# The end of a two-layer decoder kernel: last attention group transposed earlier, last norms on VectorE, clip gate by the exponential, gated rows quantised in pairs of chunks without GpSimd

## The chip, the cores and the metric

The kernel runs on one core of a Trainium2 chip. The metric is the device time of one execution in microseconds (us). The time given for a kernel is the median of several runs.

The engines go by the profile's names: PE is the matrix engine (PEld its weight loads), DVE the vector engine, ACT the scalar engine, POOL is GpSimd, and SP issues the DMAs. Each engine works off its own list of instructions in order, and waits on semaphores where it needs another's result.

## The reference

Eight sequences of 100 rows of 256 numbers pass six sublayers, each followed by a residual sum and a layer norm. Only the last two touch the change.

```python
# fifth: attention of 100 rows over 361 context rows, 16 heads of 16, with a mask
x = _layernorm(x + _L1_xattn_ref(x, ctx_1024, ctx_1024, mask, ...), axis=-1)
# sixth: feed-forward part with 8-bit fake quantisation
def _act_fake_quant(x, clip_factor):
    scale = jax.nn.sigmoid(clip_factor) * jnp.max(jnp.abs(x)) / QMAX      # QMAX = 127
    return jnp.clip(_ste_round(x / scale), -QMAX - 1.0, QMAX) * scale
xq = _act_fake_quant(x, clip_x[0])
gate = jnp.einsum('bsh,ih->bsi', xq, _weight_fake_quant(w_gate))          # 256 -> 704
up = jnp.einsum('bsh,ih->bsi', xq, _weight_fake_quant(w_up))
h = _act_fake_quant(jax.nn.silu(gate) * up, clip_down[0])
x = _layernorm(x + jnp.einsum('bsi,hi->bsh', h, _weight_fake_quant(w_down)), axis=-1)
```

Both scales need the largest absolute value over all 800 rows: nothing of `xq` exists before the last row of the attention is normed, and nothing of the quantised `h` before the last piece of `silu(gate) * up`.

## The kernel before, in words

Everything is written out by hand for each engine. Only the end of the program matters here.

**The last attention.** 16 heads in 8 sequences make 32 groups ("quads", n = 0 to 31) of four heads. In step n PE computes the scores of quad n (`pe_scores`), then the product of probabilities and values of quad n-2 (`pe_values`), then work set by the table `AT` (keys, values, queries, output product), and last the twelve transposes of the probabilities of quad n-1 (`pe_probs`, L741) in three parts into three PSUM banks. ACT computes the exponentials of quad n (L945, one per head, with row sums) and copies the three parts of quad n-1 out of PSUM (`act_probs`, L954). When the last head of a sequence b has its sum, DVE inverts the 16 sums spread to 256 columns (`dve_inverse`, L1182 and L1183), PE turns the inverse into columns (`pe_spread`, called RS below), ACT copies it (L1047), and when the last `pe_values` of the sequence is done DVE multiplies both (`dve_context`, L1191). The output product (`pe_o`, operand `wo`), the residual sum (L1261) and the norm follow. The steps after quad 31 are n = 32 (values of 30, RS of the last sequence, transposes of 31), n = 33 (values of 31, output product, and the transposes of the quantised weights `pe_ffn_weights`, L2181 and L2190, which ACT copies out in L2237 and L2240) and n = 34 (the transposes FT of the last normed rows, L792, which ACT copies in L1039).

**A norm** is started by DVE (L618 to L620), its root is taken by POOL in six small steps (`norm_root`, L639 to L645), and it is ended by subtracting and multiplying: by DVE in `norm_end` (L652) in some places, by POOL in `norm_end_pool` (L658) in this attention.

**The feed-forward part.** The peak of a tensor over all partitions goes DVE, PE (L2197), DVE (L2324), PE, DVE (`activation_scale`, L2330 and L2332). The clip gate `clip` is the sigmoid of the two factors, taken by ACT (L2245) after the attention. DVE multiplies by the reciprocal scale and adds 12582912, which rounds, and clamps (L2351, L2352); ACT subtracts the constant again and writes bfloat16 (L2251). 16 chunks of 88 x 400 (two groups of 400 rows, eight chunks each) then pass PE (gate and up), ACT (Silu, L2257), DVE (product L2361, peak L2337). After the second peak each chunk is quantised: DVE scales and rounds (L2373), POOL clamps (L2278), ACT subtracts and writes `hq` in bfloat16 (L2263). PE starts on the first group's down product when its eight chunks are there (`f_hq`), 64 matrix products of 256 columns for 8 sequences. DVE takes the results in pairs of sequences, adds the residual and starts the norm; POOL takes the root and a shift (L2284, L2287); ACT ends the norm (L2270) and SP stores 100 KB for each sequence (L2124).

## Time and profile before

| | |
|---|---|
| runs of the kernel before, us | 1299.33, 1306.27, 1304.72; median 1304.72 |
| the profiled execution | 1300.62 us, its span 1298.9 us, mean granted PE clock 0.937 |
| busy over the span | PE 87%, DVE 82%, ACT 64%, POOL 60% |
| from the last scores (1225 us) to the end | 74 us |

The span runs from the first to the last instruction; the profiled execution's own time is 1.7 us more than its span. PEclk is the clock that PE was granted, 1.00 being 2.4 GHz and 0.50 being 1.2 GHz. The tiles `arena`, `ps`, `stat` and `x_tok` are the big SBUF arena, all of PSUM, the norm's numbers and the rows of the residual stream.

### The profile page before, as it was taken

What the parts mean: (1) busy time and instruction counts of PE and PEld (TensorE: products, weight loads), DVE (VectorE), ACT (ScalarE), POOL (GpSimd) and SP (SyncE); (2) the same over time, 40 slices, a digit from 0 to 9 for tenths busy, and PEclk for the clock granted to TensorE, in tenths of its full rate; (3) what the DMA queues carried; (4) which work ended last, traced back from release to release, by engine and by line L of the source; (5) the groups of instructions that cost most, each with busy time, mean ns of one, the idle gap of its engine ahead of it and who ended that gap; (6) DMA issues with size and microseconds to landing.
All of it is one profiled execution on the core that took longest, in us unless ns stands there. A gap on an engine that the chain in (4) does not pass through costs nothing.

```text
span 1298.9 us, 17433 instructions
## 1 busy us (share of the span) xinstructions
PE 1133.0 (87%) x5930; PEld 665.4 (51%) x5930; DVE 1060.2 (82%) x1629; ACT 831.1 (64%) x1827; POOL 785.5 (60%) x660
## 2 busy tenths in 40 slices
PE   7798988888768998998989989989997888989774
PEld 3455555544334554554545545545454556666544
DVE  4577777676699999999999999999999957675566
ACT  2455555655486677767766777677675447776754
POOL 6001111100599898998988989989999913543105
PEclk9899999979889998999998999989999899998975
DMA  6000002000510602305105024041060031010000
GB/s 209 13 12 13 12 13 73 1 1 3 205 38 10 239 1 103 118 1 196 52 1 203 17 80 169 1 179 42 1 236 1 1 83 33 17 34 2 1 2 25
DMA packets 22141, 79.13 MB, mean 61 GB/s; under 512 B 4935, under 2 KB 8847, under 8 KB 21138
## 3 DMA queue, kind: packets, MB, share of 16 engines
q1 hardware_dynamic: 22054, 78.02, 17.3%
q8 instruction: 48, 0.79, 0.3%
q14 instruction: 39, 0.32, 0.1%
HBM read 76.77 MB, written 1.24 MB: 60 GB/s over the span
## 4 chain that ended last, share of the span: by engine, by line
PE 40%; DVE 33%; POOL 11%; ACT 9%; issue 7%; DMA 0%; ACTq 0%; SPq 0%; DVEq 0%; POOLq 0%
PE ps L672 36%; DVE ps L2064 10%; POOL arena L1978 6%; DVE arena L2069 5%; DVE arena L2067 4%; PE ps L741 4%; POOL arena L1990 2%; DVE hstat L1197 2%; ACT ps L1861 2%; DVE arena L2027 2%; DVE arena L1174 1%; ACT L667 1%; ACT arena L930 1%; DVE arena L1164 1%; ACT arena L945 1%
## 5 line engine op out<-in xcount | busy, mean ns | idle before, releaser
L672 PE MATMUL ps<-arena 128*32 128x100 f32 (+8 forms) x3300 | 521.0, 386 | 71.4 <-ACT arena L930 14.8
L1978 POOL TENSOR_TENSOR arena<-arena 128x1600 f32<-128x1600 f32 x128 | 456.4, 3581 | 34.6 <-DVE ps L2064 26.4
L672 PEld LDWEIGHTS ps<-arena 128*32 128x32 f32 (+6 forms) x3300 | 263.1, 147 | 297.7 <-issue 116.3
L672 PE MATMUL ps<-arena,ident 128*128 128x400 f32 x1024 | 385.9, 527 | 29.7 <-POOL arena L1990 20.7
L1861 ACT ACTIVATE ps<-arena 128x400 f32<-128x400 f32 x512 | 282.9, 590 | 185.6 <-DVE arena L2067 152.4
L2064 DVE TENSOR_TENSOR_SCAN ps<-ps,arena 128x800 f32<-128x800 f32 x176 | 320.6, 1822 | 21.5 <-ACT ps L1861 17.5
L672 PEld LDWEIGHTS ps<-arena,ident 128*128 128x128 f32 x1024 | 201.2, 200 | 196.9 <-POOL arena L1990 29.1
L639 POOL TENSOR_SCALAR stat<-stat 100x1 f32<-100x1 f32 (+1 forms) x44 | 8.4, 190 | 394.3 <-DVE stat L620 393.4
L2067 DVE TENSOR_TENSOR arena<-ps,arena 128x800 f32<-128x800 f32 x176 | 174.3, 991 | 6.0
L1990 POOL TENSOR_TENSOR arena<-arena 128x1600 f32<-128x1600 f32 x40 | 143.1, 3577 | 16.9 <-DVE arena L2069 16.8
L2069 DVE TENSOR_TENSOR_SCAN arena<-ps,arena 128x800 f32<-128x800 f32 x80 | 140.3, 1803 | 1.4 <-ACT ps L1861 1.2
L954 ACT ACTIVATE arena<-ps 128x400 f32<-128x400 f32 x192 | 90.1, 502 | 23.3 <-PE ps L741 22.2
L945 ACT ACTIVATE arena<-arena,hstat 100x361 f32<-100x361 f32 x128 | 74.9, 588 | 39.0 <-DVE hstat L1174 39.0
L1174 DVE CUSTOM_DVE_ANT_0 arena<-ps,arena 100x361 f32<-100x361 f32 x128 | 60.6, 530 | 47.7 <-PE ps L672 47.7
L741 PE MATMUL ps<-ident,arena 100*128 100x100 f32 x768 | 93.7, 262 | 5.8 <-DVE arena L1321 2.4
L930 ACT ACTIVATE arena<-ps,hstat 100x361 f32<-100x361 f32 x128 | 71.5, 561 | 36.3 <-DVE hstat L1197 36.2
L741 PEld LDWEIGHTS ps<-ident,arena 100*128 100x128 f32 x768 | 79.2, 147 | 23.1 <-issue 9.2
L667 ACT ACT_TABLE_LOAD x65 | 83.4, 1283 | 1.1
L1197 DVE TENSOR_REDUCE hstat<-ps 100x2 f32<-100x722 f32 x64 | 57.8, 905 | 26.6 <-PE ps L672 26.2
L672 PE MATMUL ps<-wv,arena 128*128 128x256 f32 (+1 forms) x192 | 54.5, 411 | 4.0 <-DVE arena L1144 3.1
L672 PE MATMUL ps<-arena,wk 128*128 128x361 f32 x128 | 51.0, 527 | 1.5 <-ACT xm L1743 0.8
L1164 DVE TENSOR_SCALAR arena<-arena,hstat 100x361 f32<-100x361 f32 x128 | 46.5, 406 | 2.3
(196 smaller groups left out, 1023.2 us busy)
## 6 DMA issues: line engine op xcount, KB each, us to landing
arena<-bc_scratch SPq DMA_DIRECT2D x64, 800.0 KB, 6.6
arena<-in_ctxT SPq DMA_DIRECT2D x16, 361.0 KB, 4.0
arena<-in_w_in SPq DMA_DIRECT2D x4, 1024.0 KB, 5.2
arena<-in_expT SPq DMA_DIRECT2D x1, 2048.0 KB, 12.5
arena<-in_w_out SPq DMA_DIRECT2D x4, 512.0 KB, 3.1
arena<-in_mask SPq DMA_DIRECT2D x8, 141.0 KB
arena<-in_xT SPq DMA_DIRECT2D x2, 400.0 KB, 4.4
x_tok<-in_x_tok SPq DMA_DIRECT2D x1, 800.0 KB
```

Source lines behind the costliest of these rows:

```text
L667: act.add_instruction(mybir.InstLoadActFuncSet(name=nc.get_next_instruction_name(), act_func_set_id=which, engine=mybir.EngineType.Activat ...
L672: return nc.tensor.matmul(outp, lhsT, rhs, start=first, stop=last)
L741: last = nc.tensor.transpose(ps[:, a.bank(b, name), k * S:(k + 1) * S], a.es[0:S, (n * QUAD + i) % 8, kc * P:(kc + 1) * P], ident[0:S, 0:S])
L930: nc.scalar.activation(a.es[0:S, v % 8, 0:SK], ps[0:S, i, 0:SK], ACT.Exp, bias=hstat[0:S, n % 2, 0, i:i + 1], scale=1.0, accum_out=hstat[0 ...
L945: nc.scalar.activation(e, e, ACT.Exp, bias=hstat[0:S, n % 2, 0, i:i + 1], scale=-1.0, accum_out=rsum[0:S, n // QUADS % 2, sum_at(n, i)]).t ...
L954: nc.scalar.activation(a.aT[:, n % 2, r * QUAD * S:(r + 1) * QUAD * S], ps[:, a.bank(b, name), 0:QUAD * S], ACT.Copy).then_inc(a.freed(b, ...
L1861: last = nc.scalar.activation(psf[:, half_at(k) + j * GT:half_at(k) + (j + 1) * GT], delta[g][:, c], ACT.Exp, scale=aneg[:, l % 2, n:n + 1])
L1978: nc.gpsimd.tensor_tensor(bx[:, unit % BX].rearrange("p (j t) -> p j t", j=SEGMENT), bbc[:, nq].rearrange("p (j t) -> p j t", j=SEGMENT), ...
L1990: nc.gpsimd.tensor_tensor(h, h, cbc[:, nq], ALU.mult).then_inc(m_cmp, 1)
L2064: nc.vector.tensor_tensor_scan(a, a, bx[:, unit % BX, w], 0.0, ALU.mult, ALU.add).then_inc(m_scan, 1)
L2067: nc.vector.tensor_tensor(y, a, cbc[:, nq, w], ALU.mult).then_inc(m_cmd, 1)
L2069: nc.vector.tensor_tensor_scan(y, a, bx[:, unit % BX, w], 0.0, ALU.mult, ALU.add).then_inc(m_scan, 1)
```

## The change

It is four edits at the end of the program.

1. The transposes of quad 31 move from the end of step 32 to its start, ahead of the values of quad 30, on PE and on ACT; in step 31 ACT's copies of quad 30's transposes alternate with the exponentials of quad 31.
2. The last sequence's norm before the feed-forward part is ended by DVE instead of POOL, and so are the last two sequences of the output, where POOL's two shift instructions and ACT's L2270 fall away (SP waits on the new semaphore `f_ended`).
3. The clip gate becomes exp(-x) on ACT in step 8 of the attention, and 1/(1+that) in two small DVE instructions at the step of the third weight scale; the Sigmoid after the attention and its table load fall away. In the feed-forward part ACT writes both groups of `xq` before its first Silu.
4. The gated rows are quantised in 8 pieces of 88 x 800 instead of 16 of 88 x 400: DVE scales and rounds, ACT subtracts the constant and writes `hq`, and DVE clamps `hq` in bfloat16, two pieces behind. POOL has no part in it.

```diff
@@ -475,6 +475,9 @@
                     for n in LAST_QUADS:
+                        if n == B * QUADS:
+                            for r in range(KC):
+                                yield B - 1, f"T{QUADS - 1}{r}"
                         for g in quad_steps(n):
@@ -490,7 +493,7 @@
                                 yield b, "RS"
-                        if has_quad(n - 1):
+                        if has_quad(n - 1) and n < B * QUADS:
                             for r in range(KC):
@@ -870,6 +873,9 @@
                     pm_out(pe, ROUNDS - 1, n)
+                if n == B * QUADS:
+                    for r in range(KC):
+                        pe_probs(pe, a, n - 1, r)
                 if has_quad(n - 2):
@@ -892,7 +898,7 @@
                         pe_spread(pe, a, b)
-                if has_quad(n - 1):
+                if has_quad(n - 1) and n < B * QUADS:
                     for r in range(KC):
@@ -1024,6 +1030,11 @@
                         act_exp_last(act, a, g)
+                        if n == B * QUADS - 1:
+                            act_probs(act, a, n - 1, g % QUAD)
+                if n == B * QUADS:
+                    for r in range(KC):
+                        act_probs(act, a, n - 1, r)
                 for g in quad_steps(n):
@@ -1041,12 +1052,15 @@
                     act_exp_last(act, a, QUAD * n + 3)
+                if n == 2 * QUADS:
+                    act.wait_ge(ld_ffn, 16 * 4)
+                    nc.scalar.activation(clip[:, :], clip[:, :], ACT.Exp, scale=-1.0).then_inc(f_sig, 1)
                 for g in quad_steps(n):
...
                                              ACT.Copy).then_inc(a.freed(b, "RS"), 1)
-                if has_quad(n - 1):
+                if has_quad(n - 1) and n < B * QUADS - 1:
                     for r in range(KC):
@@ -1094,7 +1108,8 @@
                         norm_root(pool, b % 2)
-                        norm_end_pool(pool, b % 2, a.zt[0:S, b % 2], x_tok[:, b, :], a.x_ready)
+                        if b < B - 1:
+                            norm_end_pool(pool, b % 2, a.zt[0:S, b % 2], x_tok[:, b, :], a.x_ready)
                     if g in PIECES_AT:
@@ -1337,12 +1352,21 @@
                         dve_resid(dve, a, b)
-                        norms.ended += 1
+                        if b < B - 1:
+                            norms.ended += 1
+                        else:
+                            step(V.memset(amx_in, 0.0))
+                            step(V.memset(unround, -ROUND))
+                            norm_end(dve, b % 2, a.zt[0:S, b % 2], x_tok[:, b, :], a.x_ready)
                     for b in pre(g, AT["1Q"]):
...
                             weight_scale(dve, w)
+                    if g == PEAKS_AT[2]:
+                        dve.wait_ge(f_sig, 1)
+                        step(V.tensor_scalar(clip[:, :], clip[:, :], 1.0, None, ALU.add))
+                        step(V.reciprocal(clip[:, :], clip[:, :]))
                     if g == H * (B - 1) + 10:
@@ -2120,7 +2144,10 @@
             for b in range(B):
-                sp.wait_ge(f_out, b + 1)
+                if b < B - 2:
+                    sp.wait_ge(f_out, b + 1)
+                else:
+                    sp.wait_ge(f_ended, b - B + 3)
                 sp.dma_start(out[b], fo[0:S, b % 4]).then_inc(f_stored[b % 4], 16)
@@ -2222,7 +2250,7 @@
                 if b % GB == 0:
-                    pe.wait_ge(f_hq, IC * (b // GB + 1))
+                    pe.wait_ge(f_hq, IC // 2 * (b // GB + 1))
                 if b >= 4:
@@ -2240,29 +2268,28 @@
 
+        def chunk_pair(rows_, n):
+
+            g, c = divmod(n, IC // 2)
+            return rows_[0:IP, 2 * c:2 * c + 2, g * GT:(g + 1) * GT]
+
         def ffn_act(act):
-            act.wait_ge(ld_ffn, 16 * 4)
-            nc.scalar.activation(clip[:, :], clip[:, :], ACT.Sigmoid).then_inc(f_sig, 1)
             table(act, SET_SILU)
+            for g in range(G):
+                act.wait_ge(f_xr, g + 1)
+                nc.scalar.activation(xqT[:, :, g * GT:(g + 1) * GT], xT5[:, :, g * GT:(g + 1) * GT], ACT.Identity,
+                                     bias=unround, scale=1.0).then_inc(f_xq, 1)
+            act.wait_ge(f_sg, 1)
             for n in range(FU):
-                if n in (0, 2):
-                    g = n // 2
-                    act.wait_ge(f_xr, g + 1)
-                    nc.scalar.activation(xqT[:, :, g * GT:(g + 1) * GT], xT5[:, :, g * GT:(g + 1) * GT], ACT.Identity,
-                                         bias=unround, scale=1.0).then_inc(f_xq, 1)
-                if n == 0:
-                    act.wait_ge(f_sg, 1)
                 act.wait_ge(f_gu, n + 1)
...
                                      scale=sg[:, n % IC:n % IC + 1]).then_inc(f_sil, 1)
-            for n in range(FU):
-                g, c = divmod(n, IC)
-                t = slice(g * GT, (g + 1) * GT)
-                act.wait_ge(f_r2, n + 1)
-                nc.scalar.activation(hq[0:IP, c, t], hh[0:IP, c, t], ACT.Identity, bias=unround[0:IP],
-                                     scale=1.0).then_inc(f_hq, 1)
-            for b in range(B):
+            for n in range(FU // 2):
+                act.wait_ge(f_r1, n + 1)
+                nc.scalar.activation(chunk_pair(hq, n), chunk_pair(hh, n), ACT.Identity, bias=unround[0:IP],
+                                     scale=1.0).then_inc(f_r2, 1)
+            for b in range(B - 2):
                 act.wait_ge(f_shift, b // 2 + 1)
@@ -2271,14 +2298,10 @@
         def ffn_pool(pool):
-            for n in range(FU):
-                g, c = divmod(n, IC)
-                t = slice(g * GT, (g + 1) * GT)
-                pool.wait_ge(f_r1, n + 1)
-                nc.gpsimd.tensor_scalar(hh[0:IP, c, t], hh[0:IP, c, t], ROUND + QMAX, ROUND - QMAX - 1, ALU.min,
-                                        ALU.max).then_inc(f_r2, 1)
             for p in range(B // 2):
                 norm_root(pool, 2 * p, 2, stat8)
+                if p == B // 2 - 1:
+                    break
                 st = stat8[0:S, 2 * p:2 * p + 2]
@@ -2326,7 +2349,6 @@
             dve.wait_ge(f_amaxed, k + 1)
-            dve.wait_ge(f_sig, 1)
             step(nc.vector.scalar_tensor_tensor(scale, ps[:, 7, P:P + 1], 1.0 / QMAX, clip[:, k:k + 1], ALU.mult,
@@ -2339,8 +2361,7 @@
             V = nc.vector
-            step(V.memset(amx_in, 0.0))
-            step(V.memset(unround, -ROUND))
+            dve.wait_ge(attn[1].out_ready, B)
             V.tensor_reduce(amx_in[0:S, 0:1], axm[0:S, :], AX.X, ALU.max).then_inc(f_amax, 1)
@@ -2367,10 +2388,14 @@
             activation_scale(dve, 1, shx, rhx)
-            for n in range(FU):
-                g, c = divmod(n, IC)
-                h = hh[0:IP, c, g * GT:(g + 1) * GT]
-                V.tensor_scalar(h, h, rhx[0:IP], ROUND, ALU.mult, ALU.add).then_inc(f_r1, 1)
+            for n in range(FU // 2 + 2):
+                if n < FU // 2:
+                    h = chunk_pair(hh, n)
+                    V.tensor_scalar(h, h, rhx[0:IP], ROUND, ALU.mult, ALU.add).then_inc(f_r1, 1)
+                if n >= 2:
+                    dve.wait_ge(f_r2, n - 1)
+                    h = chunk_pair(hq, n - 2)
+                    V.tensor_scalar(h, h, QMAX, -QMAX - 1, ALU.min, ALU.max).then_inc(f_hq, 1)
             dve.wait_ge(f_sdb, 1)
@@ -2385,6 +2410,12 @@
                     norm_start(2 * p + b, z[:, b], b == 1, stat8)
+            for b in (B - 2, B - 1):
+                st = stat8[0:S, b]
+                dve.wait_ge(n_root, norms.begun)
+                dve.wait_ge(f_stored[b % 4], 16 * (b // 4))
+                V.tensor_scalar(fo[0:S, b % 4], zpair[b // 2 % 3][:, b % 2], st[:, 6:7], st[:, 9:10], ALU.subtract,
+                                ALU.mult).then_inc(f_ended, 1)
 
```

**Where the instructions stand.** First PE from the scores of quad 31 on (before: L672 100x361 are scores, L672 32x100 values, L741 transposes of probabilities, L792 the turned rows FT, L672 128x100 with `ident` the RS product). Before:

```order
L672 MATMUL ps<-arena 100x361 x4
L672 MATMUL ps<-arena 32x100 x12
L741 MATMUL ps<-ident,arena 128x100 x12
L672 MATMUL ps<-arena 32x100 x12
L792 MATMUL ps<-ident,x_tok 128x100 x2
L672 MATMUL ps<-ident,arena 128x100 x2
L741 MATMUL ps<-ident,arena 128x100 x12
L672 MATMUL ps<-arena 32x100 x12
L672 MATMUL ps<-wo,arena 100x256 x2
```

After, from the same place (L675 is the old L672, L744 the old L741, L795 the old L792):

```order
L675 MATMUL ps<-arena 100x361 x4
L675 MATMUL ps<-arena 32x100 x12
L744 MATMUL ps<-ident,arena 128x100 x24
L675 MATMUL ps<-arena 32x100 x12
L795 MATMUL ps<-ident,x_tok 128x100 x2
L675 MATMUL ps<-ident,arena 128x100 x2
L675 MATMUL ps<-arena 32x100 x12
L675 MATMUL ps<-wo,arena 100x256 x2
```

The twelve transposes of quad 31 now follow those of quad 30 directly, so that nothing but FT and RS stands between the values of quad 30 and those of quad 31.

Second, ACT from the exponentials of quad 31 (L945) on. Before:

```order
L945 ACTIVATE arena,rsum<-arena,hstat 100x361 x4
L954 ACTIVATE arena<-ps 128x400 x3
L1039 ACTIVATE arena<-ps 128x2x100
L1047 ACTIVATE arena<-ps 128x200
L954 ACTIVATE arena<-ps 128x400 x3
L2237 ACTIVATE arena<-ps 128x704 x4
```

After (L951 is an exponential, L960 a copy of transposes, L1050 the copy of FT, L1061 that of RS):

```order
L951 ACTIVATE arena,rsum<-arena,hstat 100x361
L960 ACTIVATE arena<-ps 128x400
L951 ACTIVATE arena,rsum<-arena,hstat 100x361
L960 ACTIVATE arena<-ps 128x400
L951 ACTIVATE arena,rsum<-arena,hstat 100x361
L960 ACTIVATE arena<-ps 128x400
L951 ACTIVATE arena,rsum<-arena,hstat 100x361
L960 ACTIVATE arena<-ps 128x400 x3
L1050 ACTIVATE arena<-ps 128x2x100
L1061 ACTIVATE arena<-ps 128x200
L2265 ACTIVATE arena<-ps 128x704 x4
```

The copies of quad 30 went in between the exponentials, and the three of quad 31 moved ahead of the copies of FT and RS.

Third, DVE in the quantisation of the gated rows, from the second scale on. Before:

```order
L2330 SCALAR_TENSOR_TENSOR arena<-ps,clip 128x1
L2332 RECIPROCAL arena<-arena 128x1
L2373 TENSOR_SCALAR arena<-arena 88x400 x16
L2375 TENSOR_SCALAR arena<-ps,arena 100x256
L2381 TENSOR_TENSOR arena<-ps,arena 100x512
```

After (L2394 scales and rounds, L2398 clamps `hq`):

```order
L2352 SCALAR_TENSOR_TENSOR arena<-ps,clip 128x1
L2354 RECIPROCAL arena<-arena 128x1
L2394 TENSOR_SCALAR arena<-arena 88x2x400 x3
L2398 TENSOR_SCALAR arena<-arena 88x2x400
L2394 TENSOR_SCALAR arena<-arena 88x2x400
L2398 TENSOR_SCALAR arena<-arena 88x2x400
L2394 TENSOR_SCALAR arena<-arena 88x2x400
L2398 TENSOR_SCALAR arena<-arena 88x2x400
```

Sixteen instructions of 400 columns became eight of 800, and eight clamps of 800 columns came in between them, each of which waits for ACT.

## Rows read from the trace of the kernel before

**Rows 1.** The page's first line.

```profile
span 1298.9 us, 17433 instructions
```

**Rows 2.** Windows: busy time by engine in each stretch, then PEclk, DMA share, GB/s.

```profile
1231.30:1241.50 10.20, 9.04 (x86) 7.71 (x85) 1.44 (x6) 4.46 (x9) 1.33 (x5) 0.50 0.01 2
1245.10:1251.80 6.70, 4.52 (x15) 2.85 (x16) 3.55 (x9) 3.73 (x7) 0.00 (x0) 0.50 0.00 0
1252.00:1265.00 13.00, 10.91 (x54) 5.30 (x52) 12.78 (x26) 8.18 (x14) 0.00 (x0) 1.00 0.00 1
1276.00:1290.00 14.00, 13.87 (x64) 13.11 (x64) 10.97 (x32) 6.87 (x12) 9.33 (x25) 0.50 0.05 15
```

**Rows 3.** The chain that ended last, from 1226 us: start, duration, what.

```profile
1229.07 1.17 ACT arena L954 x3
1234.87 1.26 PE ps L672 x24
1236.57 2.03 PE ps L672 x4
1239.22 2.70 ACT arena L2237 x4
1241.93 1.83 ACT arena L2240 x2
1251.88 0.48 ACT arena L2251
1275.98 13.90 PE ps L672 x64
```

**Rows 4.** Timeline of PE and DVE: start, duration, instruction, idle before it and releaser.

```profile
1213.78 0.69 PE L672 MATMUL ps<-ident,arena 100*128 100x100 f32 x4 [3.02 <-DVE arena L1183]
1223.02 1.11 PE L672 MATMUL ps<-wo,arena 128*100 128x256 f32 x4
1230.38 0.72 PE L672 MATMUL ps<-arena 128*32 128x100 f32 x24 [2.53 <-ACT arena L954]
1229.11 0.17 DVE L1182 TENSOR_SCALAR rsum<-rsum 100x16 f32<-100x16 f32 x1 [1.13 <-ACT arena L945]
1229.31 1.75 DVE L1183 RECIPROCAL arena<-rsum 100x256 f32<-100x256 f32 x1
```

**Rows 5.** Timeline of POOL, and the source view of L652 (min/median/max ns).

```profile
1241.87 1.23 POOL L658 TENSOR_SCALAR x_tok<-arena,stat 100x256 f32<-100x256 f32 x1
L652 DVE TENSOR_SCALAR x_tok<-arena,stat x16: 402/408/414, 18.6 to 355.1; 100x256 f32<-100x256 f32 x16
```

**Rows 6.** Timeline of DVE at the two clip scales.

```profile
1245.61 0.16 DVE L2330 SCALAR_TENSOR_TENSOR arena<-ps,clip 128x1 f32<-128x1 f32 x1 [0.94 <-ACT clip L2245]
1269.56 0.16 DVE L2330 SCALAR_TENSOR_TENSOR arena<-ps,clip 128x1 f32<-128x1 f32 x1 [0.67 <-PE ps L672]
```

**Rows 7.** Timeline of DVE at 1246 us and from 1268 us.

```profile
1246.67 0.58 DVE L2352 TENSOR_SCALAR arena<-arena 128x800 f32<-128x800 f32 x1
1247.16 0.22 DVE L2354 TENSOR_SCALAR arena<-arena 88x8 f32<-88x8 f32 x1
1269.95 9.10 DVE L2373 TENSOR_SCALAR arena<-arena 88x400 f32<-88x400 f32 x16
```

**Rows 8.** Groups by line and form, 1244 to 1299 us: busy, mean ns.

```profile
L2263 ACT ACTIVATE arena<-arena 88x400 bf16<-88x400 f32 x16 | 9.6, 628 | 5.5 <-POOL arena L2278 5.5
L2251 ACT ACTIVATE arena<-arena 128x800 bf16<-128x800 f32 x2 | 1.9, 955 | 0.5 <-DVE arena L2352 0.5
```

**Rows 9.** Timeline of POOL and ACT in the closing norms.

```profile
1285.79 0.19 POOL L639 TENSOR_SCALAR stat<-stat 100x2 f32<-100x2 f32 x1
1292.62 0.19 POOL L639 TENSOR_SCALAR stat<-stat 100x2 f32<-100x2 f32 x1 [0.41 <-DVE stat L620]
1294.49 0.20 POOL L645 TENSOR_TENSOR stat<-stat 100x2 f32<-100x2 f32 x1
1295.28 1.09 ACT L2270 ACTIVATE arena<-arena,stat 100x256 f32<-100x256 f32 x2 [1.95 <-POOL stat L2287]
```

More of the change, by code:

```diff
@@ L2161, in decoder @@
         f_mean, f_shift = sem("f_mean"), sem("f_shift")
+        f_ended = sem("f_ended")
         f_scaled, f_round, f_clamp = sem("f_scaled"), sem("f_round"), sem("f_clamp")
```

## The prediction

> **What bounds the kernel now.** I read three kinds of view in this order. The page gives the span [rows 1]; the profiled execution took 1300.62 us, and all sums below are made against that. It lies 4.1 us under the median of the runs, 1304.72. The chain of waits says which work set the end, and from 1226 us on it consists only of what the four edits touch [rows 3]. The windows show PE's clock, which changes several times there [rows 2]. The reader is to see that this end is a relay: every piece waits for the one before, so a microsecond taken from a link of the chain is a microsecond off the time, and one taken beside it is nothing. The rest of the program keeps its instructions, but for one tiny ACT instruction and two tiny DVE ones, so the forecast is a sum over the last 74 us.
>
> **Edit 1, the last group's transposes.** Before, ACT copied quad 30's transposes after the last exponential (1229.07, 1.17 us for three), PE did the values of quad 30, FT and RS, and only then the transposes of quad 31; its values could start at 1234.87, were done 1.26 us later, then came the context product (DVE) and the output product at 1236.57, which took 2.03 us, and at 1239.22 ACT began on the weights [rows 3]. After: the three copies go in between the exponentials. They are 1.17 us of ACT in the chain, so the last exponential ends about 1.2 us later. Each part of quad 31's transposes follows its exponentials and is copied at once; ACT is through with them by about 1231.6. These no longer bind. What is late next is the inverse of the sums, which waited for the last exponential: its first instruction started at 1229.11 [rows 4], now at 1230.3. It ends 0.20 + 1.75 us later, at 1232.3 [rows 4]. RS needs it and stands ahead of quad 31's values on PE: RS took 0.69 us directly after an inverse at full clock [rows 4], so the values start at 1233.0.
>
> From here the clock decides. At full clock the 24 passes of the values take 0.72 us and the output product 0.93 of its 1.11 us before the next instruction starts [rows 4]; at half clock 1.26 and 2.03 [rows 3]. From the end of the values to the output product it was 0.44 us (1236.13 to 1236.57), and from the end of the output product to ACT's start 0.62, for eight transposes at half clock [rows 3]; at full I take 0.4 for the latter. Full: values to 1233.75, output product 1234.2 to 1235.15, ACT on the weights at 1235.6: 3.6 us earlier than 1239.22. Half: RS some 0.4 longer, values to 1234.75, output product 1235.2 to 1237.2, ACT at 1237.85: 1.4 us earlier. Before, PE had stood still for 2.53 us up to 1230.38 [rows 4], and the clock was 0.50 from 1231.3 to 1241.5 [rows 2]. Another stop of 3.02 us ended at 1213.78 [rows 4]. Now PE has pieces of quad 31's transposes to do in that stop, and by the times above no gap over 0.7 us is left between 1228.4 and 1234. I take full clock, **3.6 us**, and keep 1.4 as the lower end.
>
> **Edit 2a, the norm of the last sequence.** POOL's 1.23 us become 0.40 on DVE [rows 5]. But ACT, which must copy the turned rows, is busy with the weights until 1243.76 (2.70 and 1.83 us from 1239.22 [rows 3]), while the turned rows were there at about 1243.5 (the norm's end, 1241.87 + 1.23 [rows 5], and 0.4 of PE). The cover is ACT's weight copies, and they move together with the norm, since both hang on the output product. Worth 0 to 0.1; I take 0. If the weight copies were not there, it would be worth 0.8. The two memsets in front of it are hidden behind POOL's root.
>
> **Edit 3, the clip gate and the order of ACT.** DVE's first scale waited for the gate up to 1245.61, 0.94 us after the partition maximum; at the second scale, where the gate was long there, the same wait was 0.67, for PE [rows 6]. So the Sigmoid with its table loads cost 0.27 us and not all that it lasted; I take **0.3**. The new Exp sits in the attention, where ACT waits in every quad, and DVE's two small instructions (0.16 each [rows 6]) likewise: 0, at most 0.5 together if they hit the chain. Writing the second group of `xq` before the first Silu takes 0.48 us out of the chain at 1251.88 [rows 3], but PE's third chunk then ends only 0.25 us before the old start of its Silu: **0.2**.
>
> **Edit 4, the quantisation.** Before: DVE starts at 1269.95 [rows 7], PE at 1275.98 [rows 3], 6.03 us for eight chunks through three engines, paced by all three at 0.57 to 0.60 us a chunk (9.10 us for DVE's 16 [rows 7], 9.6 for ACT's [rows 8]). After: a piece of 800 columns is two chunks. DVE: 0.58 us, the next instruction starting after 0.49 [rows 7]. ACT: 955 ns for 800 columns [rows 8], with the next starting earlier; by its weight copies, 704 columns every 0.66 us and 1024 every 0.91 [rows 3], I estimate 0.73 us. The first piece leaves ACT 0.67 + 0.96 = 1.63 after the start, the fourth 3 x 0.73 later, at 3.82. The clamp of bfloat16 in SBUF is not in this trace. Its nearest row is DVE's float32 clamp of the same shape, 0.58 [rows 7]. Call c the time from a clamp's start to the next instruction. DVE does clamp 0 at 1.66 at the earliest, then three scalings and four clamps in turn: the group is ready at 1.66 + 3 x 0.49 + 4c. With c = 0.49 this is 5.1, and with the latency 5.2; with c = 0.28 or less, ACT's 3.82 and one clamp bind, and it is 4.4. I take 4.5, nearer the fast end because half the bytes pass: **1.5 us**, bounds 0.8 and 1.65. The Trainium skill (VectorE: DVE Perf Modes, "The perf-mode tier table") gives a tensor_scalar on bfloat16 in SBUF twice the speed of the float32 one; by it c would be near 0.28, an estimate, and the gain 1.65. The down product then runs 13.90 us at half clock [rows 3], as before; the second group is ready some 3.5 us after the first and PE comes to it after 6.9.
>
> **Edit 2b, the last output.** POOL's root ends at 1294.69 (1294.49 + 0.20), ACT starts at 1295.28 and ends both rows at 1296.37 [rows 9]. DVE now starts at 1294.73 and does two of 0.40 [rows 5], the second 0.33 after the first: 1295.47. **0.9 us**; 0.6 if the two stores, now closer together, delay each other.
>
> **Sum.** 3.6 + 0 + 0.3 + 0.2 + 1.5 + 0.9 = 6.5 us: 1294.1 for an execution like the profiled one, and 1304.72 - 6.5 = **1298.2** against the median. About 0.5%, 6.5 us, is what a measurement of this kernel can tell from no change, so the forecast sits on that line.
>
> **The rivals.**
>
> *A. The clock falls in the last group as before (30%).* The same at 1.4 for edit 1: 4.3 us, 1300.4. For it speaks that each of quad 31's transposes is short, and that PE waits for the inverse again around 1232.
>
> *B. The down product gets the full clock (12%).* The profile shows it busy for 13.87 of 14 us at 0.50 [rows 2], whereas in the gate and up products the clock was 0.50 until 1251.8 and 1.00 after [rows 2]. At full clock a pair would take PE 1.7 instead of 3.4; POOL's root and shift then bind, whose second pair began at 1285.79 and whose last took 2.66 to the start of ACT [rows 9]. That gives 1.7 for the first pair and 3 x 0.3 after: 2.6 more, 9.1 in all, 1295.6. The Trainium skill (TensorE: Matmul & The Clock Gate, Part 1) says that the half rate is the default and activity releases it, which would make this rival the outcome. This trace's 14 us do not agree with it.
>
> *C. The clock stays low through gate and up (8%).* Then a chunk takes PE 4 x 0.333 = 1.33 us (400 columns at 1.2 GHz) instead of the 1.0 us of DVE's pace (26 instructions, two a chunk, in 13 us [rows 2]): the 13 chunks now run at 1.00 cost 4.3 more. With edit 1 at 1.4, the sum is 4.3 - 4.3, no change: 1304.7. It can happen because the whole end slides forward by a few microseconds against the moments at which the clock is set.
>
> *D. The clamp is slow (3%), the one that ends slower.* Place: DVE in the quantisation. Its eight clamps and the five scalings behind the first of them end at 1.66 + 5 x 0.49 + 8c after its start, the row scale 0.5 later, and then come four pairs at 2.7 each (1289.88, PE's end, to 1292.62, POOL's start [rows 3, 9]): 15.4 + 8c. By PE's course it is 3.2 + 4c + 13.9 + 2.7, which binds below c = 1.1. Before it was 6.03 + 13.9 + 2.7 = 22.6. The other edits give 5.0, so from c = 1.53 the end is later than before; with c = 2.0 it is 31.4 - 22.6 - 5.0 = 3.8 us slower, 1308.5. Nothing in rows 7 speaks for it.
>
> *The change does nothing that can be seen (2%):* something at the start of the last group takes back edit 1, 2.9 us, 1301.8.
>
> **Numbers.** The forecast has 45%; A 30, B 12, C 8, D 3, nothing 2. The range holds the forecast with its bounds, A and B: 1293.0 to 1303.5. Faster by over 0.5%: half of the forecast's 45, a little more for the median's own scatter, a fifth of A, and B: 0.46. Within: 0.50. Slower: 0.04.
>
> **What would show it.** Edit 1: ACT's first weight copy 3.6 us nearer to the scores of quad 31; the inverse 1.2 us later than before against the scores; PEclk 1.00 at the output product. Edit 3: the first scale 0.67 us after the maximum. Edit 4: PE's down product 4.5 us after DVE's first scaling instead of 6.03, clamps of 0.35 us. Edit 2b: first store of the last pair 0.75 us earlier after POOL's root. The forecast is wrong if the clock in the down product or in the gate products differs from before, or if RS is not what the last values wait for.

## The result, and the profile after

| | before | after |
|---|---|---|
| median of 20 runs each, us | 1300.64 (1296.16 to 1308.97) | 1297.07 (1291.83 to 1302.77) |
| ratio to before | | 0.9962, 95% interval 0.9944 to 0.9981 |
| the profiled execution, its span | 1300.62, 1298.9 | 1302.77, 1301.0 |
| from quad 31's first DVE instruction to the end of the span | 72.83 | 67.06 |

Faster by 0.38%, between 2.5 and 7.3 us of 1300.64 by the interval. The profiled execution of after is longer than that of before, although its end is 5.8 us shorter. So the first thing to see is where the two differ ahead of the change. One window of 100 us of each kernel, of before and then of after (busy time and count of each engine, PEclk, DMA share, GB/s):

```profile
300.00:400.00 100.00, 78.39 (x342) 39.69 (x339) 79.43 (x112) 61.18 (x130) 59.71 (x46) 0.91 0.22 80
```

```profile
300.00:400.00 100.00, 77.85 (x326) 39.04 (x325) 69.06 (x108) 55.78 (x121) 50.53 (x49) 0.85 0.22 80
```

Both programs have the same instructions in this stretch, but the granted clock differs; the counts differ because the execution of after is behind by then. By the times of the 48 norms (DVE's aggregates), the profiled execution of after was 5.1 us late after 76 us and 11.0 late after the 23rd, at 342 us; 7.9 are left at the last scores. I therefore read all profiles from one landmark just ahead of the change: DVE's first instruction on quad 31's scores, at 1226.07 before and at 1233.94 after. From there to the end I cut the time into links, at starts that the rows show: ACT's first weight copy, DVE's first and second clip scale, the end of the span.

| link, us | before [rows 1, 3, 6] | after |
|---|---|---|
| scores to weight copy | 13.15 | 9.50 |
| to the first scale | 6.39 | 6.21 |
| to the second scale | 23.95 | 24.38 |
| to the down product | 6.42 | 5.03 |
| down product and to the end | 22.92 | 21.94 |

After, timeline of PE (start, duration, instruction, idle before it and releaser; 18 transposes are those of quad 30 and six of quad 31):

```profile
1234.47 2.54 PE L744 MATMUL ps<-ident,arena 100*128 100x100 f32 x18
1237.19 0.70 PE L744 MATMUL ps<-ident,arena 100*128 100x100 f32 x3 [0.18 <-ACT arena L951]
1238.16 0.48 PE L744 MATMUL ps<-ident,arena 100*128 100x100 f32 x3 [0.27 <-ACT arena L951]
1238.56 0.72 PE L675 MATMUL ps<-arena 128*32 128x100 f32 x24
1240.15 0.69 PE L675 MATMUL ps<-ident,arena 100*128 100x100 f32 x4 [0.55 <-DVE arena L1198]
1240.77 0.72 PE L675 MATMUL ps<-arena 128*32 128x100 f32 x24
1241.98 1.11 PE L675 MATMUL ps<-wo,arena 128*100 128x256 f32 x4 [0.49 <-DVE arena L1206]
1279.06 13.89 PE L675 MATMUL ps<-arena 88*100 88x256 bf16 x64 [5.07 <-DVE arena L2398]
```

After, timelines of DVE and ACT:

```profile
1238.35 1.75 DVE L1198 RECIPROCAL arena<-rsum 100x256 f32<-100x256 f32 x1
1249.65 0.16 DVE L2352 SCALAR_TENSOR_TENSOR arena<-ps,clip 128x1 f32<-128x1 f32 x1 [0.67 <-PE ps L675]
1274.03 0.16 DVE L2352 SCALAR_TENSOR_TENSOR arena<-ps,clip 128x1 f32<-128x1 f32 x1 [0.67 <-PE ps L675]
1274.42 1.72 DVE L2394 TENSOR_SCALAR arena<-arena 88x800 f32<-88x800 f32 x3
1278.64 0.37 DVE L2398 TENSOR_SCALAR arena<-arena 88x800 bf16<-88x800 bf16 x1
1282.84 0.69 DVE L2406 TENSOR_TENSOR arena<-ps,arena 100x512 f32<-100x512 f32 x1
1297.81 0.74 DVE L2417 TENSOR_SCALAR arena<-arena,stat 100x256 f32<-100x256 f32 x2 [2.19 <-POOL stat L648]
1243.44 2.71 ACT L2265 ACTIVATE arena<-ps 128x704 bf16<-128x704 bf16 x4 [2.23 <-PE ps L2209]
1275.08 6.93 ACT L2290 ACTIVATE arena<-arena 88x800 bf16<-88x800 f32 x8 [5.06 <-DVE arena L2394]
```

After, windows of the last group, the gate and up products (12.6 us of them, and their first 5.94), and the down product:

```profile
1234.00:1242.00 8.00, 6.32 (x103) 4.37 (x95) 4.41 (x12) 5.45 (x16) 2.05 (x6) 1.00 0.01 3
1254.40:1267.00 12.60, 11.40 (x50) 6.16 (x49) 11.22 (x22) 7.32 (x13) 0.00 (x0) 0.84 0.01 3
1252.43:1258.37 5.94, 5.94 (x18) 3.54 (x19) 3.09 (x6) 3.10 (x5) 0.00 (x0) 0.50 0.00 0
1278.80:1292.80 14.00, 13.74 (x64) 13.21 (x64) 10.47 (x32) 5.19 (x8) 5.46 (x18) 0.50 0.05 15
```

Against before: PE's stop of 2.53 us [rows 4] is gone, no stop over 0.55 us is left in its place, the values and the output product ran at full clock (0.72 and 1.11 instead of 1.26 and 2.03 [rows 3]), the first scale waits 0.67 us, for PE, instead of 0.94 for ACT [rows 6], and the down product starts 4.64 us after DVE's first scaling instead of 6.03 [rows 3, 7]. But in the gate and up products the clock was at 0.50 for longer. Both kernels start them 2.78 us after the first scale; after ran their first 5.94 us at half clock, before only the first 3.5; from 1252 us on it had 1.00 [rows 2]. The window of before:

```profile
1248.39:1251.86 3.47, 3.47 (x11) 2.11 (x12) 0.90 (x2) 1.16 (x3) 0.00 (x0) 0.50 0.00 0
```

By the prediction's own last sentence, a clock in the gate products that differs from before is a sign that the forecast is wrong. It is taken up below.

### The profile page after: what moved, and what is told of

It reads as the page before. It is cut to its first block, busy times and chain, and to the rows that moved or that the text cites. A ratio compares the mean times of both kernels' runs of the same rounds, so it can differ in the third digit from the quotient of the medians.

```text
span 1301.0 us, 17408 instructions
## 1 busy us (share of the span) xinstructions
PE 1135.5 (87%) x5930; PEld 666.2 (51%) x5930; DVE 1059.7 (81%) x1634; ACT 826.2 (64%) x1816; POOL 775.3 (60%) x641
## 4 chain that ended last, share of the span: by engine, by line
PE 42%; DVE 33%; ACT 9%; POOL 7%; issue 7%; DMA 1%; SPq 0%; DVEq 0%; POOLq 0%; ACTq 0%
PE ps L675 38%; DVE ps L2088 10%; DVE arena L2093 5%; DVE arena L2091 5%; POOL arena L2002 4%; PE ps L744 4%; ACT ps L1885 2%; DVE hstat L1212 2%; POOL arena L2014 2%; DVE arena L2051 2%; DVE arena L1189 1%; ACT L670 1%; ACT arena L936 1%; DVE arena L1198 1%; DMA arena<-in_exb 1%
## 5 line engine op out<-in xcount | busy, mean ns | idle before, releaser
L675 PE MATMUL ps<-arena 128*32 128x100 f32 (+8 forms) x3300 | 521.3, 384 | 68.1 <-ACT arena L936 15.1
L675 PEld LDWEIGHTS ps<-arena 128*32 128x32 f32 (+6 forms) x3300 | 263.7, 147 | 292.8 <-issue 113.2
L675 PE MATMUL ps<-arena,ident 128*128 128x400 f32 x1024 | 385.5, 527 | 29.4 <-POOL arena L2014 19.9
L675 PEld LDWEIGHTS ps<-arena,ident 128*128 128x128 f32 x1024 | 201.6, 200 | 196.4 <-issue 28.6
L960 ACT ACTIVATE arena<-ps 128x400 f32<-128x400 f32 x192 | 90.1, 502 | 24.9 <-PE ps L744 23.8
L744 PE MATMUL ps<-ident,arena 100*128 100x100 f32 x768 | 94.2, 261 | 8.2 <-DVE arena L1336 3.7
L951 ACT ACTIVATE arena<-arena,hstat 100x361 f32<-100x361 f32 x128 | 75.0, 588 | 39.3 <-DVE hstat L1189 39.3
L744 PEld LDWEIGHTS ps<-ident,arena 100*128 100x128 f32 x768 | 78.8, 146 | 27.0 <-issue 9.8
L675 PE MATMUL ps<-wv,arena 128*128 128x256 f32 (+1 forms) x192 | 54.7, 412 | 4.1 <-DVE arena L1159 3.3
L675 PE MATMUL ps<-arena,wk 128*128 128x361 f32 x128 | 51.0, 527 | 1.5 <-ACT xm L1767 0.8
```

Of the source, the lines that this page charges most:

```text
L675: return nc.tensor.matmul(outp, lhsT, rhs, start=first, stop=last)
L744: last = nc.tensor.transpose(ps[:, a.bank(b, name), k * S:(k + 1) * S], a.es[0:S, (n * QUAD + i) % 8, kc * P:(kc + 1) * P], ident[0:S, 0:S])
L960: nc.scalar.activation(a.aT[:, n % 2, r * QUAD * S:(r + 1) * QUAD * S], ps[:, a.bank(b, name), 0:QUAD * S], ACT.Copy).then_inc(a.freed(b, ...
```

## The experiments

Times are cut from the same landmark; "end" is from the second scale to the end of the span, and "clock" the granted clock from the landmark to the end of the output product ("falls" where it drops to 0.50 on the way). Each row is one profiled execution. Beside x1 to x8 the kernel before took 1302.01 us, beside x12 1305.76. Single times differ by as much as 13 us between executions of one kernel, so the links are what is compared, and the time only where there are several runs.

| kernel | to weight copy | to 1st scale | to 2nd scale | end | sum | clock | its time |
|---|---|---|---|---|---|---|---|
| before | 13.15 | 6.39 | 23.95 | 29.34 | 72.83 | falls | 1300.62 |
| after | 9.50 | 6.21 | 24.38 | 26.97 | 67.06 | 1.00 | 1302.77 |
| x1_order | 11.81 | 6.39 | 23.76 | 29.30 | 71.26 | falls | 1297.04 |
| x2_busy | 10.28 | 6.59 | 24.05 | 29.32 | 70.24 | 1.00 | 1303.72 |
| x3_quant | 13.36 | 6.37 | 23.96 | 27.96 | 71.65 | falls | 1305.19 |
| x4_single | 9.51 | 6.20 | 24.38 | 27.56 | 67.65 | 1.00 | 1297.27 |
| x5_gpsimd | 11.49 | 6.10 | 23.64 | 28.67 | 69.90 | falls | 1296.54 |
| x6_no2a3 | 11.20 | 6.40 | 23.49 | 27.00 | 68.09 | falls | 1294.19 |
| x7_warmgate | 11.53 | 5.89 | 22.61 | 27.00 | 67.03 | falls | 1298.02 |
| x8_warmdown | 9.51 | 6.20 | 23.60 | 25.37 | 64.68 | 1.00 | 1291.45 |
| x9_both | 9.50 | 5.90 | 22.31 | 25.37 | 63.08 | 1.00 | 1290.36 |
| x10_same | 9.51 | 6.20 | 24.38 | 26.96 | 67.05 | 1.00 | 1297.75 |
| x11_three | 9.50 | 5.90 | 22.31 | 25.40 | 63.11 | 1.00 | 1290.04 |
| x12_gpsimd_again | 11.52 | 5.90 | 23.75 | 28.76 | 69.93 | falls | 1301.17 |

**Edit 1 alone (x1_order).** The kernel before, with the hunks of edit 1 and no other:

```diff
+                if n == B * QUADS:
+                    for r in range(KC):
+                        pe_probs(pe, a, n - 1, r)
                 if has_quad(n - 2):
...
-                if has_quad(n - 1):
+                if has_quad(n - 1) and n < B * QUADS:
```

> The kernel before with edit 1 alone (the order of quad 31's transposes). Measured in the profile from DVE's first instruction on quad 31's scores to ACT's first copy of the weight transposes: 13.15 us before, 9.50 after. The theory of links says that this part needs nothing of the other edits: 9.5 here, and all later links as before (6.4 to the first clip scale, 6.4 from the second clip scale to the down product, 9.0 from its end to the end). The rival, that part of the gain came from the other edits (VectorE's norm, the missing Sigmoid), says 10.5 or more.

Measured: 11.81 instead of the 9.5 expected, 1.34 us off the first link, and nothing off the others by more than 0.2. That is the number of the rival, 10.5 or more, but not its reason: the clock fell. PE's timeline of this kernel, and the output product of x12_gpsimd_again, which has all of edits 1 to 3 and in which the clock fell too:

```profile
1230.45 1.09 PE L675 MATMUL ps<-ident,arena 100*128 100x100 f32 x4
1231.48 1.23 PE L675 MATMUL ps<-arena 128*32 128x100 f32 x24
1233.20 2.02 PE L675 MATMUL ps<-wo,arena 128*100 128x256 f32 x4 [0.49 <-DVE arena L1202]
```

```profile
1238.74 2.00 PE L675 MATMUL ps<-wo,arena 128*100 128x256 f32 x4 [0.49 <-DVE arena L1206]
```

The output product starts 9.16 us after the landmark here (1224.04) and 9.17 there (1229.57). So the other edits give this link nothing.

The course is rival A of the prediction by each of its steps: RS 0.4 longer than 0.69, values 1.23, output product 2.02.

**The clock alone (x2_busy).** The order of before, and PE given idle work in its stop after quad 31's scores:

```diff
+                if n == B * QUADS:
+                    pe.wait_ge(a.max_ready, B * H)
+                    keep(4, 0, ident[:, :], wq[:, 0, :], P, D)   # 4 products nobody reads
                 if has_quad(n - 2):
```

> The kernel before, order unchanged, but PE is given four idle 128x256 float32 products (results unused, in a PSUM bank that is free by then) in its stop of 2.5 us ahead of quad 30's values. If 2.2 of edit 1's 3.65 us are the clock, the granted clock stays at 1.00 where it was 0.50, and scores to weight copies fall from 13.15 to 10.5 to 11.5 us. If the gain is the order's alone, they stay at 13.0 or above although the products run.

Measured: the clock was 1.00 over the whole group and the link 10.28, a little below the 10.5 to 11.5 expected: 2.87 us are the clock's in the old order. Windows of this kernel, from its scores on:

```profile
1231.76:1246.00 14.24, 10.58 (x162) 8.55 (x157) 5.50 (x16) 9.52 (x22) 4.67 (x13) 1.00 0.01 2
```

At full clock the new order is worth 10.28 - 9.50 = 0.78, at half clock 1.34 to 1.95 (13.15 to 11.81 and to 11.20). How edit 1's 3.65 us divide depends on which comes first: 2.87 for the clock and 0.78 for the order, or 1.3 to 2.0 for the order and the rest for the clock. In both, the clock is about half or more.

**Edit 4 alone (x3_quant).** The quantisation of after in the kernel before:

```diff
-            for n in range(FU):
+            for n in range(FU // 2 + 2):
+                if n < FU // 2:
+                    h = chunk_pair(hh, n)
+                    V.tensor_scalar(h, h, rhx[0:IP], ROUND, ALU.mult, ALU.add).then_inc(f_r1, 1)
+                if n >= 2:
+                    dve.wait_ge(f_r2, n - 1)
+                    h = chunk_pair(hq, n - 2)
+                    V.tensor_scalar(h, h, QMAX, -QMAX - 1, ALU.min, ALU.max).then_inc(f_hq, 1)
```

> The kernel before with edit 4 alone (quantisation in eight pieces, no GpSimd). From the second clip scale to the first down product: 6.42 us before, 5.03 after. The theory of links says 5.0 here and every other link as before. The rival, that DVE's and PE's later links give it back because the second group of pieces comes late, says a stop of PE in the middle of the down product, which then lasts longer than 13.9 us.

Measured: from the second scale to the down product 5.03, where before had 6.42: 1.39 us, to the hundredth what the whole change shows there. The down product took 13.89 us as before, without the rival's stop. From its start to the end are 22.93 us here and 21.94 after; only edit 2b lies between them, so the 0.99 are its.

**Size of the pieces (x4_single).** After, with 16 pieces of 400 columns:

```diff
-            for n in range(FU // 2 + 2):
-                if n < FU // 2:
+            for n in range(FU + 3):
+                if n < FU:
```

> The changed kernel with 16 pieces of 88x400 instead of eight of 88x800 in the quantisation, still without GpSimd (VectorE scales, ScalarE subtracts, VectorE clamps in bfloat16 three pieces behind). From the second clip scale to the down product: 5.03 us with pairs, 6.42 before. If the size of the pieces brings the gain, 16 fixed costs come back: 5.8 to 6.5. If leaving GpSimd out brings it, the time stays at 4.8 to 5.2, because each chunk costs ScalarE 0.42 us and VectorE 0.33 + 0.2.

**Who clamps (x5_gpsimd, x12_gpsimd_again).** After, with pieces of 800 columns, clamped by GpSimd in float32 between DVE and ACT:

```diff
+            for n in range(FU // 2):
+                pool.wait_ge(f_r1, n + 1)
+                nc.gpsimd.tensor_scalar(chunk_pair(hh, n), chunk_pair(hh, n), ROUND + QMAX, ROUND - QMAX - 1,
+                                        ALU.min, ALU.max).then_inc(f_r2, 1)
```

> The changed kernel with eight pieces of 88x800, but clamped by GpSimd in float32 between VectorE and ScalarE, as the kernel before did with 16. If the size of the pieces brings the gain, the second clip scale to the down product takes about 5.2 us; if GpSimd is what costs, 6.0 or more, since a piece then passes three engines in turn (0.64 + 1.0 + 0.96 us for the first) and GpSimd takes about 1.0 us for each of the next three.

Measured from the second scale to the down product: 5.63 in x4_single, 6.75 in both runs with GpSimd. The 5.63 lie between the two ranges expected: of edit 4's 1.39 us, 0.79 come with leaving GpSimd out at the old size, and 0.60 more with the larger pieces. Large pieces with GpSimd give back 1.72, more than all of edit 4, and are 0.33 slower than before. What the engines did stands in three timelines, of x4_single, and of x5_gpsimd twice (DVE, POOL):

```profile
1268.33 1.44 DVE L2394 TENSOR_SCALAR arena<-arena 88x400 f32<-88x400 f32 x4
1268.79 8.42 ACT L2290 ACTIVATE arena<-arena 88x400 bf16<-88x400 f32 x16 [4.85 <-DVE arena L2394]
```

```profile
1266.53 8.01 DVE L2398 TENSOR_SCALAR arena<-arena 88x800 f32<-88x800 f32 x8
1267.25 8.92 POOL L2303 TENSOR_SCALAR arena<-arena 88x800 f32<-88x800 f32 x8 [28.32 <-DVE arena L2398]
```

DVE scales four chunks in 1.44 us without GpSimd, 0.34 from one start to the next; before, with GpSimd beside it, 16 took 9.10 [rows 7], 0.57 each. For 800 columns it is 0.55 alone (1.72 for three) and with GpSimd 1.00 on the average of eight, 1.15 once both are at work. So DVE's 0.57 us before was not its own pace: it had GpSimd beside it. The Trainium skill (SBUF - State Buffer, "Who interferes with whom") has it that a DVE tensor_scalar in a two-port mode and a GpSimd instruction lock each other out of a shared pair of ports for a whole instruction; the paces agree with it. It is not DVE that the down product waits for in x5_gpsimd, though. It waits for ACT's fourth piece, and that waits for GpSimd's fourth; GpSimd's pieces also follow each other about 1.15 us apart there (the last one, with DVE done, took 0.85). How much of the 1.72 us is the third engine in the row and how much the sharing was not told apart. In x4_single ACT's pieces came every 0.52 us, not the 0.42 expected, and DVE's scaling with its clamp every 0.51, and seven such steps lie ahead of the eighth chunk.

**The last norm and the gate (x6_no2a3).** After, with the norm of the last sequence ended by POOL and the Sigmoid after the attention, as before:

```diff
-                        if b < B - 1:
-                            norm_end_pool(pool, b % 2, a.zt[0:S, b % 2], x_tok[:, b, :], a.x_ready)
+                        norm_end_pool(pool, b % 2, a.zt[0:S, b % 2], x_tok[:, b, :], a.x_ready)
...
+            nc.scalar.activation(clip[:, :], clip[:, :], ACT.Sigmoid).then_inc(f_sig, 1)
             table(act, SET_SILU)
```

> The changed kernel without two of its parts: the last norm before the feed-forward part is ended by GpSimd again, and the gate is ACT's Sigmoid with its table load again (the order of ACT's xq writes stays changed). The theory of links says that these parts are worth 0.2 to 0.4 us together: from the first weight copy to the first clip scale 6.2 becomes 6.4 to 6.6, since ACT's weight copies cover the norm. The rival, that the norm was on the path, says 7.0 or more.

Measured: the link to the first scale is 6.40, that of before; the first scale waits 0.94 us for the gate again. The two edits together are worth 0.2 us.

**Clock in the gate products (x7_warmgate).** After, with idle products of 88 x 400 ahead of the gate and up products (16 in four places, two of which are shown, `keep` as above):

```diff
             pe.wait_ge(f_wtc, 6)
+            keep(6, 4, wgT[:, 0, 0:IP], wgT[:, 0, 0:GT], IP, GT)
+            pe.wait_ge(f_xr, 1)
+            keep(4, 4, wgT[:, 0, 0:IP], wgT[:, 0, 0:GT], IP, GT)
```

> The changed kernel with 16 idle products of 88x400 in bfloat16 (results unused) on PE in its stops between the weight transposes and the gate products. The clock is to be 1.00 at the first gate product instead of 0.50. First to second clip scale: 24.38 us after, 23.95 before. If the low clock is what makes the first chunks late, it becomes 22.0 to 22.8; if VectorE's pace alone sets it, 23.8 or more.

Measured: the link between the scales is 22.61, 1.77 less than after, within the first range expected. In this execution the clock fell in the last group, which cost 2.03, so the sum is that of after by chance.

**Clock in the down product (x8_warmdown).** After, with idle products during the quantisation:

```diff
             pe.wait_ge(f_sil, FU)
+            keep(6, 0, wgT[:, 0, 0:IP], wgT[:, 0, 0:GT], IP, GT)
...
+            for k in range(3):
+                pe.wait_ge(f_hq, k + 1)
+                keep(3, 0, wgT[:, 0, 0:IP], wgT[:, 0, 0:GT], IP, GT)
```

> The changed kernel with 24 idle products of 88x400 in bfloat16 (results unused) on PE between the last gate product and the down product, in small groups that follow the quantisation. Rival B of the prediction: the down product falls from 13.89 us to 9 to 12 (then VectorE, GpSimd and the free PSUM banks bind), and the total from the last scores by 2 to 3 us. If this stream of 88-row products runs at the low clock whatever was before it, the clock is 1.00 at its start and 0.50 soon after, and it takes 12 us or more.

Measured: the down product ran at full clock, which it does in no kernel without these products: 8.0 us from its first product to its last instead of 13.9 (9 to 12 expected), and 16 of its 64 in 1.95 us instead of a quarter of 13.89. The sum is 2.38 us below that of after, within the 2 to 3 expected, but 0.78 of this lie between the scales, where the clock came up 3.3 us earlier than in after and nothing was edited. Timelines of PE, POOL and POOL again:

```profile
1276.41 1.95 PE L675 MATMUL ps<-arena 88*100 88x256 bf16 x16 [0.50 <-DVE arena L2418]
1275.87 0.19 POOL L642 TENSOR_SCALAR stat<-stat 100x2 f32<-100x2 f32 x1 [38.53 <-DVE stat L623]
1278.60 0.19 POOL L642 TENSOR_SCALAR stat<-stat 100x2 f32<-100x2 f32 x1
1281.33 0.19 POOL L642 TENSOR_SCALAR stat<-stat 100x2 f32<-100x2 f32 x1
```

POOL's pairs now follow each other without idle time, 2.73 us apart, the last after 3.10: it binds, as rival B said. But the link from the second scale to the end is only 1.60 us shorter, not 2.6. After, DVE took up the first pair 8.81 us after the second scale (1282.84 - 1274.03), for its clamps last until then; with the fast product it is no earlier (8.82 in x9_both). Only the three later pairs gain, from 3.4 to 2.85 each on the average.

**Both (x9_both) and all three (x11_three).** After with the idle products of x7 and x8, and then with those of x2 too:

```diff
+                    pe.wait_ge(a.max_ready, B * H)      # x11_three only
+                    keep(4, 0, ident[:, :], wq[:, 0, :], P, D)
```

> The changed kernel with both sets of idle matrix products, before the gate and up products and during the quantisation; nothing else differs. Theory (the clock at the start of the down product is what it keeps): the gate and up stage runs at full clock from its first chunk, the two clip scales lie about 22.6 us apart instead of 24.4, the down product starts at clock 1.00 and ends before POOL's work does, and from quad 31's scores to the end it is 67.1 - 1.8 - 2.4 = 62.9 us; the time about 4 us below the changed kernel and 8 below the kernel before, ratio to before near 0.993. Rival (the idle products only shift the moments at which the clock drops, and both gains exclude each other): the down product is back at 0.50 and the total stays at 65 to 67 us.

> The changed kernel with the two sets of idle products and with four more, 128 by 256 in float32, in PE's stop after quad 31's scores, so that PE isn't idle there either. Theory: the clock is 1.00 through the whole end; the link from the scores to ACT's first weight copy is 9.5 us, the gate and up stage 22.6, the down product as in the run with idle products in the quantisation, in all 62.9 us or somewhat under, and the time within 0.1 per cent of that with two sets if that one's last group is at full clock too, 2 us under it if not. Rival (the four products delay quad 31's transposes by themselves): the link to the first weight copy is 10 us or more with the clock at 1.00.

> The changed kernel once more, without any edit, to see what repeats. Theory (with the same order of code the clock in the last group differs from execution to execution, which makes 2 us of the first edit come or go): the link from quad 31's scores to ACT's first weight copy is 9.5 us if the clock there is 1.00 and 11.3 to 11.5 if it falls; all other links repeat within 0.1 us, apart from the gate and up stage, which takes 24.4 in the first case and 23.5 in the second. Rival (the clock follows the code, and the other experiments moved it by their edits): 9.50 and 24.38 again. The ratio to the kernel before should be near 0.996 by either.

| | runs | median, us | ratio to before (1301.02, 13 runs) |
|---|---|---|---|
| x10_same | 8 | 1295.47 | 0.9969 (0.9944 to 0.9994) |
| x9_both | 6 | 1290.61 | 0.9936 (0.9915 to 0.9957) |
| x11_three | 6 | 1291.38 | 0.9935 (0.9916 to 0.9955) |

Both gains add up: 63.08 us where 62.9 was expected, 3.98 below after. Windows of x9_both, from the last scores to the last products of the gate, and the quantisation with the down product:

```profile
1225.50:1262.50 37.00, 29.16 (x250) 17.35 (x249) 26.31 (x64) 22.55 (x42) 3.65 (x12) 1.00 0.01 2
1262.50:1277.30 14.80, 12.43 (x84) 9.63 (x84) 12.94 (x37) 6.93 (x8) 1.96 (x8) 0.88 0.01 1
```

The third set adds nothing, since the clock was up already. The median of x9_both lies 10.4 us below that of the kernel before and 4.9 below that of the changed kernel in the same series, though the two intervals just overlap. x10_same repeated the links of after within 0.02 us, which spoke for its rival, that the clock follows the code. So one more run went to a kernel whose edit lies some 30 us behind the last group and in whose first profile the clock had fallen:

> The kernel with GpSimd's clamp in the quantisation once more, without any edit. Its edit lies some 30 us behind the last attention group, and yet its first profile had the clock fall in that group (11.49 us from quad 31's scores to ACT's first weight copy), where the changed kernel had 1.00 and 9.50 twice. Theory A (the clock there differs from execution to execution): 9.5 or 11.5, and 9.5 would settle it. Theory B (it follows the code, by some way that isn't seen): 11.49 within 0.05 again. The quantisation's link repeats at 6.75 within 0.05 by both.

Measured: 11.52. By the letter that is theory B. But the rows are not the same. First x5_gpsimd, then x12_gpsimd_again, timeline of PE, the values of quad 30 and RS:

```profile
1229.53 0.72 PE L675 MATMUL ps<-arena 128*32 128x100 f32 x24
1231.11 0.98 PE L675 MATMUL ps<-ident,arena 100*128 100x100 f32 x4 [0.54 <-DVE arena L1198]
```

```profile
1234.49 1.23 PE L675 MATMUL ps<-arena 128*32 128x100 f32 x24
1236.03 1.06 PE L675 MATMUL ps<-ident,arena 100*128 100x100 f32 x4
```

The values of quad 30 were at full clock in the first and at half in the second: the clock fell some 2 us earlier against the scores, in front of a stretch that doesn't bind. That the course of the clock differs between executions of one code is shown; that it makes the difference between 9.50 and 11.5 for one and the same kernel is not. It was 1.00 in six and fell in four of the ten profiles of after and its variants.

Two things in the traces speak for theory A all the same. x7_warmgate and x9_both have the same instructions up to the last gate and up product, and in the first the clock fell (11.53), in the second it did not (9.50). And one number sorts the ten profiles: how long before the landmark the clock had last come up (in after, it was 0.50 until 1227.6 and 1.00 from 1227.7 on). It was 6.15 to 6.33 us in the six, and 6.04, 6.06, 6.81 and 7.20 us in the four. That was found by sorting rows after the runs and no run sets it, so it is a hint and not a cause.

## Why the prediction was right

The forecast was 1298.2 in a range of 1293.0 to 1303.5, with 0.50 for within 0.5% and 0.46 for faster. The median is 1297.07, and the ratio of 0.9962 lies within 0.5%. From the landmark to the end the sum was 6.5 us and measured 5.77. Step by step:

- **Edit 1, 3.6 us: right, 3.65.** The inverse starts 4.20 us after the landmark (1238.14), before 3.04: 1.16 later, forecast 1.2. RS 0.69, values 0.72, output product 1.11 are the forecast's rows at full clock. But its other case is as real: the same order took 11.2 to 11.8 us in five profiles, with 1.34 in x1_order against the forecast's 1.4. Full clock was taken "since no gap over 0.7 us is left"; x5_gpsimd and x12_gpsimd_again have no longer gap either and lost it. So that reason is not sufficient. Rival A had 30% and came in four of the ten profiles of after and its variants.
- **Edits 2a and 3, 0 and 0.3: 0.18** (x6_no2a3: 0.2). The wait at the first scale shrank from 0.94 to 0.67, as expected. The 0.67 is itself a number of the half clock: in the profiles whose link is 5.9 it is 0.47.
- **The stage between the scales, 0.2 shorter: the step that failed.** It is 0.43 longer. The forecast added the order of `xq` to a stage whose clock it took to be that of before, and named another clock in the gate products as a sign of being wrong; it gave that 8%, as rival C. The order is not what failed. No run changes it alone, but x3_quant (old order) and x5_gpsimd (new order) had the clock at 0.50 for nearly as long, the first 3.06 and 3.13 us of the gate products, and took 23.96 and 23.64: 0.32 less with the new order. After has the order of x5_gpsimd and 5.94 us at 0.50, and took 24.38: 0.74 more. With the clock up throughout it is 22.31. ACT's first Silus came 1.27 to 1.34 us apart, PE's pace at 1.2 GHz (1.33 by rival C), and not 1.0. So rival C's mechanism came for the first four or so chunks and not for all, and cost tenths of its 4.3 us.

Windows of x3_quant and of x5_gpsimd, from the first gate product to the rise of the clock:

```profile
1254.36:1257.42 3.06, 3.06 (x10) 1.80 (x11) 0.91 (x2) 0.75 (x2) 0.00 (x0) 0.50 0.00 0
```

```profile
1245.28:1248.41 3.13, 3.13 (x10) 1.91 (x11) 0.90 (x2) 1.78 (x3) 0.00 (x0) 0.50 0.00 0
```

- **Edit 4, 1.5 us: 1.39.** The clamp was faster than taken, 0.36 us and 0.28 from its start to the next (1278.64 to 1278.92). That is the estimate made from the table of the Trainium skill (VectorE: DVE Perf Modes, "The perf-mode tier table"), and the trace agrees with it. But ACT was slower: 0.85 for a piece (6.93 for eight), not 0.73, which was taken from copies of other forms. So ACT binds, and its fourth piece comes 3 x 0.12 later.
- **Edit 2b, 0.9 us: 0.98**, and 0.99 against x3_quant.
- **Rival B** did not happen by itself, but its condition can be made (x8_warmdown) and is worth 1.60 instead of 2.6; its first pair was reckoned without DVE's clamps, which edit 4 itself puts in its way. **Rival D** is excluded by the clamp's 0.36.
- **The base.** 1298.2 was 6.5 below a median of three runs that lies 4.1 above that of twenty. The right time came partly from that, and that part is luck: 1300.64 less the 5.8 of the links would be 1294.9, and after's median is 2.2 above it. That fits executions in which the clock falls in the last group, and the scatter of a median; they are not told apart further.

## What to carry to other kernels

Read such a change from a landmark just ahead of it, in several profiled executions: here one execution was 11 us late in stages that the change doesn't touch. In this chain of short products the granted clock was a term as large as the order of the work or larger: of 3.65 us for the reordering 2.87 could be had by four idle products alone, and 40 idle products, whose results nobody reads, gave 4 us more on top of the change. Before splitting elementwise work over DVE and GpSimd, compare DVE's pace without GpSimd: taking GpSimd out left DVE with twice the columns' work and still less time (7.99 us from 1274.42 on, against 9.10).

## What was not expected of the hardware

- The down product, 64 products of 256 columns with PE busy for 13.74 to 13.87 of 14 us, stayed at 0.50 to its end in every profile in which the clock was low at its start, eleven in all, and was at full speed in each of the three where the clock was up. The Trainium skill (TensorE: Matmul & The Clock Gate, Part 1) says that activity releases the half rate; these stretches of dense work don't agree with that.
- DVE's scaling of 88 x 800 in float32 took 0.55 us from one start to the next alone and 1.00 on the average with GpSimd on the same tile; of 88 x 400, 0.34 and 0.57.
- ACT's pieces from float32 to bfloat16 follow each other every 0.85 us for 800 columns and every 0.52 for 400 (8.42 for 16).
- The profiled executions of one program started its last group up to 5 us apart (after 1233.94, x10_same 1228.95), and those of all kernels between 1224 and 1234.
